# Spreading the reciprocals of the softmax sums over 128 partitions with Pool and TensorE in place of two DMAs, in an attention and mixture-of-experts kernel

## The chip, the core and the metric

The kernel runs on one core of one Trainium2 chip. A core has five engines that work side by side, each through its own instruction stream in order: TensorE (PE, with its weight load shown as PEld), VectorE (DVE), ScalarE (ACT), GpSimd (POOL) and SyncE (SP), which here only issues transfers. Sixteen DMA engines move data between the chip's memory and the core. An instruction that waits for a semaphore holds up all that stands behind it on its engine. The metric is the device time of one execution in microseconds (us).

## What is computed

Eight sequences of 512 tokens with 512 features go through a cross-attention with 16 heads of 32 features, and then through eight experts of which each takes its 512 best tokens. Cut to what matters:

```python
def xattn(q, k, v, mask, Wq, bq, Wk, bk, Wv, bv, Wo, bo):      # b=8, s=512, n=16 heads
    qh = (q @ Wq + bq).reshape(b, s, n, -1).transpose(0, 2, 1, 3)
    kh = (k @ Wk + bk).reshape(b, k.shape[1], n, -1).transpose(0, 2, 1, 3)
    vh = (v @ Wv + bv).reshape(b, v.shape[1], n, -1).transpose(0, 2, 1, 3)
    sim = einsum('bnid,bnjd->bnij', qh, kh) * 32 ** -0.5
    sim = where(~mask[:, None, None, :], finfo.min, sim)
    out = einsum('bnij,bnjd->bnid', softmax(sim, axis=-1), vh)
    return out.transpose(0, 2, 1, 3).reshape(b, s, -1) @ Wo + bo

x = x + xattn(layernorm(x), ctx, ctx, mask, ...)
x = x + ffn(layernorm(x), ...)     # softmax router, top 512 tokens of each of 8 experts, gelu, scatter-add
```

## The kernel before

The attention is worked off in 32 **groups**: a group is one sequence and four of its 16 heads, so four groups make a batch. Below, r0 to r3 are the four groups of a batch (`r = i % GB`), and g is a group's number. What a group takes, in the order of its data:

- The q and k projections, in three matmuls a chunk for accuracy (`hi` and `lo` parts; L1550 to L1552), are written by ACT and DVE to `qT_hi`, `qT_lo`, `kT_hi`, `kT_lo`. SP stores them to memory (`keep_hi` L735, `keep_lo` L742) and loads them back, stacked on other partitions, into `kst` and `qst` (`stack_hi` L758, `stack_lo` L767). A stack of q is three transfers of 256 KB. SP issues them in order, and the loads wait for the stores.
- Sixteen matmuls of kind `max` (L1564, tokens on partitions) give the scores of four heads and four token tiles. DVE takes each row's extreme (`nmax`, L1195), and ACT takes exp with its sum in `den` (`sum`, L1018). These wait for `qst` and `kst`.
- `rows`: PE turns the maxima to rows (L1571), ACT and DVE write them into `by_row` (L1009, L1203), and POOL copies them with two transfers into `qst` (`rows_lo`, L933).
- Sixteen matmuls of kind `score` (L1584, keys on partitions) give the scores again, with the maxima already subtracted. ACT takes exp (L1030), and four `att` steps multiply with v into `ps_att` (L1595).
- The sums' reciprocals are needed on the partitions of `ps_att`: head h and feature d on partition 32h + d, tokens along the free axis. `den` holds them as 128 tokens by 16 (head, tile). DVE takes the reciprocal (`recip`, L1211), PE turns it to 16 rows (`rden`, L1577), DVE copies the rows (L1218), POOL stores them to memory (`rden_rows`, L915), and POOL loads them back, each row for 32 partitions (`rden_in`, L924: 256 KB into `rden_b`). `divide` (L1228) multiplies `ps_att` with `rden_b` into `att_n`, which `osplit` turns into `oT_hi` and `oT_lo` for the output projection (L1611 to L1613).

Group i's scores run beside the maxima of group i + 1 and the projections of group i + 2. In between come the loads of the next sequence (r1), the first half of the output projection with its residual loads and `add_bias` on POOL (r2, L868 and L875), and the second half with the stores of x1, its normalisation and its routing (r0 of the next batch: `out`, `x1_norm`, `route`, `logits`, `back`; L1623 is the transposes of `route`).

The order is set by hand in `attention_agenda`: a group's time is cut into parts of 1/20, and a table gives the place at which each kind of step is put, as a fraction of a group (`K_AT`, `MAX_AT`, ...). PE works in that order. The other engines sort the same steps by their time plus a lag of their own (`a.lags`). Seven PSUM banks are given out in turn, so a step also waits until its bank has been emptied. After the attention comes the expert phase, which no part of the change touches.

## Time and profile before

| | |
|---|---|
| median of 3 runs | 1830.25 us (1829.41 to 1837.01) |
| the profiled execution, its own time | 1843.59 us |
| its span from first to last instruction | 1841.8 us |
| attention, between two like places of batches 0 and 7 (143.8 to 1012.0) | 868.2 us |
| PE, DVE, ACT busy in it | 774.5, 578.2, 668.5 us |
| experts (1090.0 to the end) | 751.8 us |

The profile lists for every engine how long it was busy, what it waited for, and which transfers it issued. PE's clock has two levels here, 1.2 and 2.4 GHz. The column PEclk is the mean granted clock as a share of the higher one, so 0.50 is a stretch wholly at 1.2 GHz. A wait "<-issue" is idle time for which the profile names no releaser.

### The profile page before, as it was taken

The page shows a single profiled execution, that of the slowest core. Times are in us where ns is not written, and L with a number is a line of the kernel's source. Part 1 is how long each engine was busy: PE and PEld are TensorE (multiplying, and loading weights), DVE is VectorE, ACT ScalarE, POOL GpSimd, SP SyncE. Part 2 cuts the span into 40 slices and gives each one's busy share as a digit, 9 for nine tenths or more (in the row PEclk, how much of TensorE's full clock was granted, in tenths as well). Part 3 has the DMA queues.
Part 4 walks back from the last instruction along what each step waited for, and adds up shares of the span by engine and source line. Part 5 has one row for each costly group of instructions (what it writes and reads, how often), then busy time and mean ns, then how long its engine had stood idle before and what let it go on. Part 6 is the DMA issues. An engine that isn't in the chain of part 4 may idle for free.

```text
span 1841.8 us, 22009 instructions
## 1 busy us (share of the span) xinstructions
PE 1642.2 (89%) x7667; PEld 1168.1 (63%) x7667; DVE 1112.4 (60%) x1950; ACT 982.2 (53%) x2111; POOL 309.1 (17%) x409
## 2 busy tenths in 40 slices
PE   4789989889789899898898629999999999999996
PEld 3545646546456456465564318878888888888885
DVE  5575775766656756767666455776544455554543
ACT  2687787778677776878878412222222232232321
POOL 3122121220221221212212111010202020202101
PEclk9789989889789899999998859999999999999998
DMA  5445462643644454627445122243425251525231
GB/s 187 127 125 143 132 165 73 195 111 104 179 112 126 149 133 134 164 79 213 118 136 156 65 80 89 72 121 115 146 89 166 69 166 69 166 71 178 86 107 23
DMA packets 142375, 227.53 MB, mean 124 GB/s; under 512 B 24380, under 2 KB 58832, under 8 KB 142264
## 3 DMA queue, kind: packets, MB, share of 16 engines
q1 hardware_dynamic: 115960, 175.85, 31.1%
q0 software_dynamic: 26304, 50.27, 10.7%
q8 instruction: 61, 1.00, 0.2%
q14 instruction: 50, 0.41, 0.1%
HBM read 166.36 MB, written 59.13 MB: 122 GB/s over the span
## 4 chain that ended last, share of the span: by engine, by line
PE 71%; DMA 12%; DVE 6%; ACT 6%; issue 3%; POOL 1%; SPq 0%; ACTq 0%; POOLq 0%; DVEq 0%
PE ps_gen L679 8%; PE ps_gen L680 8%; PE ps_gen L681 8%; PE ps_gen L1737 6%; PE ps_gen L1738 6%; PE ps_gen L1739 6%; PE ps_gen L1564 5%; PE ps_att L1595 5%; PE ps_gen L1584 4%; DMA qst<-qk_rows 4%; PE ps_gen L1550 3%; PE ps_gen L1551 3%; PE ps_gen L1552 3%; ACT ps_gen L1018 3%; DMA qk_rows<-qT_hi 2%
## 5 line engine op out<-in xcount | busy, mean ns | idle before, releaser
L1195 DVE TENSOR_REDUCE nmax<-ps_gen 128x1 f32<-128x512 f32 x512 | 340.3, 684 | 176.7 <-PE ps_gen L1564 172.1
L1030 ACT ACTIVATE p_ring<-ps_gen,keep_scale 128x512 f32<-128x512 f32 x512 | 336.3, 691 | 103.3 <-PE ps_gen L1584 103.2
L1018 ACT ACTIVATE ps_gen<-ps_gen,nmax 128x512 f32<-128x512 f32 x512 | 342.5, 672 | 90.1 <-DVE nmax L1195 89.8
L1080 ACT ACTIVATE gel<-ps_gen,b_cols 128x512 f32<-128x512 f32 x128 | 88.3, 690 | 451.4 <-PE ps_gen L681 451.3
L1564 PE MATMUL ps_gen<-kst,qst 97*128 97x512 f32 x512 | 226.6, 467 | 59.6 <-issue 30.0
L1449 DVE TENSOR_TENSOR gel_lo<-gel,gel_hi 128x512 fp32r<-128x512 f32 x126 | 87.2, 692 | 288.9 <-ACT gel_hi L1081 288.9
L1584 PE MATMUL ps_gen<-qst,kst 99*128 99x512 f32 x512 | 203.6, 449 | 26.5 <-ACT ps_gen L1018 13.7
L1564 PEld LDWEIGHTS ps_gen<-kst,qst 97*128 97x128 f32 x512 | 106.6, 212 | 157.3 <-issue 88.8
L679 PE MATMUL ps_gen<-hT_hi,w_hi 128*128 128x512 f32 x512 | 203.7, 398 | 1.5 <-DVE hT_lo L1442 1.5
L681 PE MATMUL ps_gen<-hT_hi,w_lo 128*128 128x512 f32 x512 | 200.8, 392 | 0.0
L680 PE MATMUL ps_gen<-hT_lo,w_hi 128*128 128x512 f32 x512 | 200.6, 392 | 0.0
L1737 PE MATMUL ps_gen<-w_hi,gel_hi 128*128 128x512 f32 x504 | 198.4, 394 | 0.0
L1739 PE MATMUL ps_gen<-w_hi,gel_lo 128*128 128x512 f32 x504 | 196.7, 390 | 0.0
L1738 PE MATMUL ps_gen<-w_lo,gel_hi 128*128 128x512 f32 x504 | 196.6, 390 | 0.0
L1595 PE MATMUL ps_att<-p_ring,v_sb 128*32 128x512 f32 x1024 | 154.2, 677 | 6.3 <-ACT p_ring L1030 6.3
L1584 PEld LDWEIGHTS ps_gen<-qst,kst 99*128 99x128 f32 x512 | 97.8, 206 | 90.0 <-issue 46.6
L959 POOL DMA_INDIRECT out_x<-y_out,idx x32 | 55.7, 1742 | 583.2 <-ACT y_out L1100 504.7
L1018 ACT ACTIVATION_READ_ACCUMULATOR ps_gen<-ps_gen,nmax 128x1 f32 x512 | 111.5, 218 | 0.0
L679 PEld LDWEIGHTS ps_gen<-hT_hi,w_hi 128*128 128x128 f32 x512 | 96.9, 189 | 21.2 <-issue 1.9
L681 PEld LDWEIGHTS ps_gen<-hT_hi,w_lo 128*128 128x128 f32 x512 | 96.8, 189 | 20.8
L680 PEld LDWEIGHTS ps_gen<-hT_lo,w_hi 128*128 128x128 f32 x512 | 97.0, 189 | 19.2
L1739 PEld LDWEIGHTS ps_gen<-w_hi,gel_lo 128*128 128x128 f32 x504 | 94.7, 188 | 19.8
(194 smaller groups left out, 2638.2 us busy)
## 6 DMA issues: line engine op xcount, KB each, us to landing
w_raw<-in_L_ffn_W SPq DMA_DIRECT2D x128, 512.0 KB, 5.0
kst<-qk_rows SPq DMA_DIRECT2D x96, 256.0 KB, 4.1
qst<-qk_rows SPq DMA_DIRECT2D x96, 256.0 KB, 4.7
x_in<-in_x POOLq DMA_DIRECT2D x60, 256.0 KB, 5.0
qk_rows<-kT_hi SPq DMA_DIRECT2D x32, 256.0 KB, 2.0
qk_rows<-kT_lo SPq DMA_DIRECT2D x32, 256.0 KB, 2.0
qk_rows<-qT_hi SPq DMA_DIRECT2D x32, 256.0 KB, 3.6
qk_rows<-qT_lo SPq DMA_DIRECT2D x32, 256.0 KB, 3.6
```

The source lines that it names most:

```text
L679: e.matmul(psum, lhsT=wh, rhs=mh, start=(i == 0), stop=False)
L680: e.matmul(psum, lhsT=wh, rhs=ml, start=False, stop=False)
L681: last = e.matmul(psum, lhsT=wl, rhs=mh, start=False, stop=(i == n - 1))
L1018: e.activation(psum[:, :], psum[:, :], ACT.Exp, bias=nmax[g % 2][:, c], scale=-1.0, accum_out=den[g % 2][:, c]).then_inc(drained_sem("max" ...
L1030: e.activation(p_ring[n % NP_][:, :], ps("score", g, kt, h)[:, :], ACT.Exp, scale=keep_scale[:, b:b + 1]).then_inc(drained_sem("score", g, ...
L1195: e.tensor_reduce(nmax[g % 2][:, h * TB + t:h * TB + t + 1], ps("max", g, h, t)[:, :], AX.X, ALU.min).then_inc(s_min, 1)
L1564: e.matmul(ps("max", g, h, t)[:, :], lhsT=qst[k][0:ROWS_MAX, h, t * P:(t + 1) * P], rhs=kst[k][0:ROWS_MAX, h, :], start=True, stop=True).t ...
L1584: e.matmul(ps("score", g, kt, h)[:, :], lhsT=kst[k][0:ROWS_ALL, h, kt * P:(kt + 1) * P], rhs=qst[k][0:ROWS_ALL, h, :], start=True, stop=Tr ...
L1595: last = e.matmul(ps_att[h * DH:(h + 1) * DH, :], lhsT=v_sb[:, kt, (c4 * HG + h) * DH:(c4 * HG + h + 1) * DH], rhs=p_ring[((g * KT + kt) * ...
L1737: e.matmul(ps_y[tt], lhsT=gh, rhs=wh, start=(j == 0), stop=False)
L1738: e.matmul(ps_y[tt], lhsT=gh, rhs=wl, start=False, stop=False)
L1739: return e.matmul(ps_y[tt], lhsT=gl, rhs=wh, start=False, stop=(j == NF - 1))
```

## The change

Three things are changed.

First, the reciprocals no longer go through memory. POOL copies `rden` (128 tokens by 16) into a new tile `rden_wide` (128 by 4 by 128) and repeats each element 32 times along the free axis. PE then turns its four 128x128 blocks by transposes, and since each head's value stands 32 times along the free axis, it now stands on 32 partitions. DVE copies the whole bank of 128x512 into `att_n`, and `divide` reads and writes `att_n` in place. `rden_b`, `rden_rows`, both transfers of each group and the semaphores `s_rd_out` and `s_rd_in` are gone.

Second, there are other waits: `recip` on DVE waits for POOL's copy of the group before, POOL's copy waits for `recip`, PE's transposes wait for POOL's copy, and DVE's copy waits for `osplit_lo` of the group before, since it overwrites `att_n`.

Third, the places and lags of the table are set anew.

```diff
-    ROWS_AT = 0.74
-    RECIP_AT, RDEN_AT, RDEN_IN_AT, OSPLIT_AT = -0.07, 0.28, 0.63, 0.17
+    ROWS_AT = 0.70
+    RECIP_AT, RDEN_AT, OSPLIT_AT = 0.02, 0.50, 0.15
-    LOAD_X_AT, STATS_X_AT = (0.32, 0.63), (0.62, 0.99)
+    LOAD_X_AT, STATS_X_AT = (0.12, 0.47), (0.65, 0.96)
-    HALF_AT, HALF_FOR = (("residual", 0.20), ("add_bias", 0.35), ("outa", 0.49)), 0.78
+    HALF_AT, HALF_FOR = (("residual", 0.05), ("add_bias", 0.23), ("outa", 0.48)), 0.78
...
-        place(i, (RDEN_IN_AT, RDEN_IN_AT), [(a.add, "rden_in", i)])
...
-        rden_b = sb(p1, "rden_b", [P, S])
+        rden_wide = sb(p1, "rden_wide", [P, TB, P])
...
+                elif kind == "recip":
+                    g, = at
+                    on.wait_ge(s_ones_rows[NST - 1], 2)
+                    on.wait_ge(s_rden, g + 1)
+                    if g > 0:
+                        on.wait_ge(*full("rden", g - 1))
+                    e.tensor_copy(rden_wide[:, :, :].rearrange("p t (h d) -> p t h d", d=DH),
+                                  rden[:, :].rearrange("p (h t d) -> p t h d", t=TB, d=1).to_broadcast([P, TB, HG, DH])
+                                  ).then_inc(s_rden_wide, 1)
...
-                elif kind == "rden":
-                    g, = at
-                    on.wait_ge(*drained("rden", g))
-                    if g >= 2:
-                        on.wait_ge(s_rd_in, 16 * (g - 1))
-                    e.dma_start(rden_rows[g % 2].rearrange("h (t n) -> (h t) n", n=P), rd_rows).then_inc(s_rd_out, 16)
-
-                elif kind == "rden_in":
-                    g, = at
-                    on.wait_ge(s_rd_out, 16 * (g + 1))
-                    on.wait_ge(s_mask_store, 16)
-                    if g > 0:
-                        on.wait_ge(s_nrm, g)
-                    src = rden_rows[g % 2].rearrange("h (r n) -> h r n", r=1).to_broadcast([HG, DH, S])
-                    e.dma_start(rden_b[:, :], src).then_inc(s_rd_in, 16)
...
-                    if g > 0:
-                        on.wait_ge(s_rd_out, 16 * g)
-                    e.tensor_copy(rd_rows, ps("rden", g)[0:HG * TB, 0:P]).then_inc(drained_sem("rden", g), 1)
+                    if g == 0:
+                        on.wait_ge(s_mask_store, 16)
+                    else:
+                        on.wait_ge(s_ol, g)
+                    e.tensor_copy(att_n[:, :], ps("rden", g)[:, :]).then_inc(drained_sem("rden", g), 1)
...
-                    on.wait_ge(s_rd_in, 16 * (g + 1))
-                    if g > 0:
-                        on.wait_ge(s_oh, g)
-                        on.wait_ge(s_ol, g)
-                    e.tensor_tensor(att_n[:, :], ps_att[:, :], rden_b[:, :], ALU.mult).then_inc(s_nrm, 1)
+                    on.wait_ge(*drained("rden", g))
+                    e.tensor_tensor(att_n[:, :], ps_att[:, :], att_n[:, :], ALU.mult).then_inc(s_nrm, 1)
...
-                    on.wait_ge(s_rden, g + 1)
-                    e.transpose(ps("rden", g)[0:HG * TB, 0:P], rden[:, :], ident[:, :]).then_inc(full_sem("rden", g), 1)
+                    on.wait_ge(s_rden_wide, g + 1)
+                    for t in range(TB):
+                        last = e.transpose(ps("rden", g)[:, t * P:(t + 1) * P], rden_wide[:, t, :], ident[:, :])
+                    last.then_inc(full_sem("rden", g), 1)
```

On POOL, in r2 of the first batch, the order before was this (`x_in<-in_x` is a residual load, `x_in<-x_in,bo_b` its `add_bias`, `qst<-by_row` is `rows_lo`):

```order
L868 DMA x_in<-in_x 128x512
L915 DMA rden_rows<-by_row 16x128
L875 TENSOR_TENSOR x_in<-x_in,bo_b 128x512
L868 DMA x_in<-in_x 128x512
L924 DMA rden_b<-rden_rows 128x1x512
L875 TENSOR_TENSOR x_in<-x_in,bo_b 128x512
L868 DMA x_in<-in_x 128x512
L933 DMA qst<-by_row 1x16x128 x2
L875 TENSOR_TENSOR x_in<-x_in,bo_b 128x512
```

At the same place it is now this:

```order
L873 COPY rden_wide<-rden 128x512
L865 DMA x_in<-in_x 128x512
L882 TENSOR_TENSOR x_in<-x_in,bo_b 128x512
L865 DMA x_in<-in_x 128x512
L882 TENSOR_TENSOR x_in<-x_in,bo_b 128x512
L865 DMA x_in<-in_x 128x512
L882 TENSOR_TENSOR x_in<-x_in,bo_b 128x512
L924 DMA qst<-by_row 1x16x128 x2
```

The copy stands ahead of the residual loads, both transfers of the reciprocals are gone from between them, and the third `add_bias` now comes ahead of `rows_lo`.

On PE, in r2 of the fifth batch, this is what followed the last q projection (first row) before. `ps_gen<-qst,kst` is a `score`, `ps_gen<-kst,qst` a `max` of the next group:

```order
L1552 MATMUL ps_gen<-xT_hi,wq_lo 128x512
L1584 MATMUL ps_gen<-qst,kst 128x512
L1564 MATMUL ps_gen<-kst,qst 128x512
L1584 MATMUL ps_gen<-qst,kst 128x512
L1564 MATMUL ps_gen<-kst,qst 128x512 x2
L1584 MATMUL ps_gen<-qst,kst 128x512 x2
L1564 MATMUL ps_gen<-kst,qst 128x512
L1595 MATMUL ps_att<-p_ring,v_sb 32x512 x4
L1564 MATMUL ps_gen<-kst,qst 128x512
```

Now it is this:

```order
L1542 MATMUL ps_gen<-xT_hi,wq_lo 128x512
L1554 MATMUL ps_gen<-kst,qst 128x512
L1576 MATMUL ps_gen<-qst,kst 128x512
L1554 MATMUL ps_gen<-kst,qst 128x512 x2
L1576 MATMUL ps_gen<-qst,kst 128x512
L1554 MATMUL ps_gen<-kst,qst 128x512 x2
L1576 MATMUL ps_gen<-qst,kst 128x512 x2
L1568 MATMUL ps_gen<-ident,rden_wide 128x128 x4
L1554 MATMUL ps_gen<-kst,qst 128x512
L1587 MATMUL ps_att<-p_ring,v_sb 32x512 x4
L1554 MATMUL ps_gen<-kst,qst 128x512
```

The last q projection is two `max` matmuls earlier in the order, and the four transposes stand behind it, where before the single one stood ahead of it. What comes after these rows, up to the first `max` for which PE needs the stack of this q, is the same in both.

## Rows read from the trace of the kernel before

**Rows 1.** The page's part 1: busy time by engine, its share of the span.

```profile
PE 1642.2 (89%) x7667; PEld 1168.1 (63%) x7667; DVE 1112.4 (60%) x1950; ACT 982.2 (53%) x2111; POOL 309.1 (17%) x409
```

**Rows 2.** Windows: stretch, its us, busy PE, PEld, DVE, ACT, POOL; PEclk, DMA share, GB/s.

```profile
143.83:1012.00 868.17, 774.51 (x3650) 482.85 (x3649) 578.18 (x1110) 668.45 (x1550) 175.57 (x286) 0.92 0.49 138
392.12:521.87 129.75, 114.62 (x526) 71.84 (x524) 84.21 (x162) 95.75 (x222) 25.49 (x41) 0.88 0.46 131
772.42:891.62 119.20, 106.29 (x526) 67.10 (x524) 83.36 (x162) 95.25 (x222) 25.31 (x41) 0.97 0.51 143
```

**Rows 3.** Waits of PE in 143.83 to 1012: us in total, times, longest.

```profile
PE ps_gen L1564 <- issue: 27.7, 14, 3.8
PE ps_gen L1564 <- ACT ps_gen L1018: 17.7, 15, 1.7
PE ps_gen L1584 <- DMA qst<-by_row: 9.7, 10, 3.0
PE ps_gen L1564 <- DMA qst<-qk_rows: 1.9, 2, 1.1
```

**Rows 4.** Timeline of PE: start, us, instruction, idle time before it.

```profile
279.14 0.77 PE L1564 MATMUL ps_gen<-kst,qst 97*128 97x512 f32 x1 [2.65 <-issue]
342.66 0.47 PE L1564 MATMUL ps_gen<-kst,qst 97*128 97x512 f32 x1 [2.20 <-issue]
406.18 0.76 PE L1564 MATMUL ps_gen<-kst,qst 97*128 97x512 f32 x1 [3.84 <-issue]
845.65 0.70 PE L1564 MATMUL ps_gen<-kst,qst 97*128 97x512 f32 x2 [1.14 <-DMA qst<-qk_rows]
```

**Rows 5.** Windows of 8 us that begin where such waits end, columns as in rows 2.

```profile
279.14:287.14 8.00, 8.00 (x22) 6.35 (x23) 3.59 (x7) 3.62 (x10) 2.13 (x3) 0.61 0.14 35
342.66:350.66 8.00, 7.68 (x25) 4.42 (x26) 4.37 (x9) 3.45 (x9) 1.70 (x3) 0.57 0.47 163
785.18:793.18 8.00, 8.00 (x37) 5.65 (x38) 5.26 (x9) 5.57 (x14) 2.60 (x3) 1.00 0.13 35
```

**Rows 6.** Timeline of POOL's and SP's queues in r2, 266 to 271.

```profile
267.37 0.70 POOL L924 DMA_DIRECT2D rden_b<-rden_rows  x1 [0.98 <-DMA rden_rows<-by_row]
...
269.88 0.80 SPq L758 DMA_DIRECT2D qst<-qk_rows  x2
```

**Rows 7.** DMA issues of 269.86 to 270.78, us to landing at the end.

```profile
qst<-qk_rows SPq DMA_DIRECT2D x3, 256.0 KB, 7.7
```

**Rows 8.** The same of 680.14 to 681.06, in r3.

```profile
qst<-qk_rows SPq DMA_DIRECT2D x3, 256.0 KB, 8.1
```

**Rows 9.** The same of 921.80 to 922.70, in r3.

```profile
qst<-qk_rows SPq DMA_DIRECT2D x3, 256.0 KB, 3.7
```

**Rows 10.** The same of 803.06 to 803.98, in r3; `rden_b` was issued at 801.58.

```profile
qst<-qk_rows SPq DMA_DIRECT2D x2, 256.0 KB, 5.8
```

**Rows 11.** Timeline of POOL's queue, issues of `rden_b` by rows 8 and 9.

```profile
679.30 0.72 POOL L924 DMA_DIRECT2D rden_b<-rden_rows  x1 [2.01 <-DMA rden_rows<-by_row]
922.48 0.72 POOL L924 DMA_DIRECT2D rden_b<-rden_rows  x1 [3.54 <-issue]
```

**Rows 12.** Timeline of PE: four transposes of 128x128, and the single one of `rden`.

```profile
610.33 0.60 PE L1623 MATMUL ps_gen<-ident,x_in 128*128 128x128 f32 x4
614.48 0.27 PE L1577 MATMUL ps_gen<-ident,rden 128*16 128x128 f32 x1
```

**Rows 13.** Groups of instructions on POOL and DVE: count, busy us, mean ns, idle before.

```profile
L875 POOL TENSOR_TENSOR x_in<-x_in,bo_b 128x512 f32<-128x512 f32 x32 | 41.0, 1281 | 43.7 <-DMA x_in<-in_x 43.4
L1245 DVE COPY hnT<-ps_gen 128x512 f32<-128x512 f32 x28 | 19.3, 689 | 22.7 <-PE ps_gen L1623 22.7
L1218 DVE COPY by_row<-ps_gen 16x128 f32<-16x128 f32 x32 | 9.0, 282 | 2.1 <-PE ps_gen L1577 0.6
```

**Rows 14.** Timeline of DVE and POOL at 15 us, where both work on SBUF.

```profile
15.17 2.11 DVE L1120 TENSOR_SCALAR x_in<-x_in,mv,rstd 128x512 f32<-128x512 f32 x1 [0.66 <-POOL rstd L811]
15.19 1.80 POOL L845 MEMSET kst<- 32x2048 f32 x1
```

41 lines of the change are left out of this document (19 added, 22 removed).

## The prediction

> **What bounds the kernel now.** I read the busy times first [rows 1]: PE is busy for 1642.2 of 1841.8 us, and every other engine for 60% or less. Then the stretch in which the change lies, by windows [rows 2]. In 868.17 us of attention PE is busy for 774.51, ACT for 668.45 and DVE for 578.18 us. So PE sets the pace there, and what can be won is its 93.7 us of idle time and what its clock costs (0.92 of full). A slow batch takes 129.75 us at clock 0.88 and a quick one 119.20 us at 0.97, with the same instructions in the same order: idle time and clock are the whole difference.
>
> Next, PE's waits in that stretch [rows 3]. The matmul at L1564 waits 27.7 us for "issue" in 14 pieces and 1.9 us for the stack transfer by name. The timeline shows where [rows 4]: at the first `max` of a group, in r2 (at 279.14 and 406.18, five more of 1.9 to 3.5 us) and in r0 (at 342.66 and 845.65, six in all, 0.8 to 2.2 us). Both lie where a stack of q has just landed: the three loads issued from 269.88 on took 7.7 us [rows 6, 7], so they landed at about 278.5, and PE went on at 279.14. I take these "issue" waits as waits for the stack. Another 9.7 us are waits for `rows_lo`. The 17.7 us at L1564 for ACT are bursts of ACT's own work in r1 and r2, and this change does not touch them.
>
> The clock comes on top. In the 8 us after such a wait it was 0.61 and 0.57, so PE spent most of them at 1.2 GHz, while ACT was busy for under 4 of the 8 us and so did not hold PE up [rows 5]. After the waits of the quick batch it stayed at 1.00. Of the twelve such windows from 279 us on, eight are below 1: together they lose 22.5 us ((1 - clock) times 8 each).
>
> **What the change removes.** No wait of `divide` on `rden_b` shows in the trace, so its transfer costs nothing by itself. What it costs is its place among other transfers. `rden_b` is issued at 267.37, 2.5 us ahead of the stack for which PE then waits [rows 6]. r3 shows the price with little else in flight: with `rden_b` issued at 679.30, ahead of the stack, the stack took 8.1 us; issued at 922.48, behind it, 3.7 us [rows 8, 9, 11]. So up to 4.4 us per stack. Another stack with it ahead took 5.8 us [rows 10], which gives 2.1 us as the low end. The waits in r2 sum to 18.9 us (seven) and those in r0 to 8.6 us (six). With 2.1 us off each, at least 14.5 and 8.5 us of them would go, 23 in all; with 4.4 us all 27.5. But residual loads in r2 and the stores of x1 in r0 remain among these transfers, so part of the relief is lost. In r2 the last q projection also moves two `max` matmuls earlier against the first matmul that needs it, which adds half a microsecond or more of slack. I take **24 us** of gain, with 10 as the low end if the remaining loads take the freed place.
>
> The waits for `rows_lo` (9.7 us) follow in the same stretches and pass POOL's queue, on which two issues per group are gone. In r1 the loads of x are placed earlier, so its normalisation no longer stands late ahead of `rows_lo`. I take **4 us**, ends 0 and 9.7.
>
> The clock: if a wait shrinks below about 1 us, the stretch after it has a chance to stay at 2.4 GHz, as after the 1.14 us at 845.65 [rows 4]. The profiled execution had 22.5 us of this loss, but its own time, 1843.59 us, is 13.3 us above the median, and I put that down to the clock. A median run then has about 9 us of it left to win, of which I take **6**; ends 0 and 22.5, the latter against the profiled run's own time.
>
> **What it adds.** On PE, four transposes stand where one did. Four of 128x128 took 0.60 us from first start to last end, one took 0.27 us [rows 12]. The difference of 0.33 us in 32 groups is **11 us**, and PE has no cover for it outside its waits. At 1.2 GHz it is near twice that, so the ends are 11 and 22. A rule of the Trainium skill speaks for a higher price: "TensorE: Matmul & The Clock Gate", section "PE-mode transpose", gives about 275 ns for one 128x128 transpose in a kernel. The single one here agrees (0.27 us), but four in a row overlap: 0.60 us, not 1.1 us. By the page's figure for each of the four the term would be 26 us instead of 11, and the forecast some 15 us later.
>
> On DVE, a copy of 689 ns takes the place of one of 282 ns [rows 13]: 0.41 us times 32 is 13 us more on an engine that is idle for a third of the stretch. It costs where DVE is late for the next `nmax`, and PE's bank is held by it: 1 us, ends 0 and 5. On POOL the copy of 128x512 is an operation the trace does not show. The nearest row is `add_bias` of that size with 1281 ns [rows 13]. It comes at 0.06 of a group and PE asks at 0.50, some 12 us later, and POOL is busy for 20% of the time, so it is hidden; only for the first group does the chain from `recip` over POOL to PE lie open. There PE waits for `rows_lo` anyway: 1 us. `divide` waits for DVE's own copy half a group earlier: nothing.
>
> **The sum.** -24 - 4 - 6 + 11 + 1 + 1 = -21 us, so 1830.25 becomes **1809 us**. The places that are moved besides shift single steps by a place or two on PE, and I give them no term.
>
> **The rivals.**
>
> *All of it comes back.* Both kinds of waits and the clock recover nearly whole: -27.5 - 9.7 - 22.5 + 13 = -46.7 against the profiled run's own time of 1843.59, so some 1797, and less for a median run whose clock also gains: 1785 to 1797. For it speaks the quick batch of 119.20 us; against it that the quick batch still had its waits, so a part of the spread between batches has another cause.
>
> *The freed place is taken.* `rden_b` is one of several transfers before each late stack. If residual loads and x1 stores now meet the stack, relief is half (-12), the clock does not recover, `rows_lo` gives nothing: -12 + 13 = +1, 1831 us, no difference that the measurement can tell. About 0.5% of the time is what it can tell.
>
> *POOL stands in DVE's way.* At 15.17 a DVE operation of this shape took 2.11 us while POOL wrote `kst` beside it [rows 14], where even a copy of that size out of PSUM takes 0.69 us [rows 13]. POOL's new copy runs at the start of each group, and in r1 and r2 a normalisation, on which the transposes for `route` and of x wait, stands close to it. If each of these 14 is held up by the 1.3 us of a copy and passes it on to PE, 18 us are lost: 1830.25 - 21 + 18 = 1827 us. "SBUF — State Buffer", section "Who interferes with whom", in the Trainium skill states this as a rule: a DVE operation in a two-port mode and one of GpSimd exclude each other for a whole instruction. The trace agrees at that one place; no row shows it inside the groups.
>
> *PE pays and wins nothing (slower).* The waits in r2 are set by the chain store, load, landing of q alone, and `rden_b`'s share is hidden behind the residual loads. Then PE carries four transposes in each group, and where the clock is at 1.2 GHz for double the price: +11 to +22 and 2 for the rest, 1843 to 1854 us. The point from which it decides is a relief of less than the price of the transposes, 0.35 to 0.7 us per group, or 1.4 to 2.8 us per batch where a batch now waits some 4 us for stacks. Against it speaks the pair in r3, for it that in r2 residual loads are in flight too.
>
> **How the numbers follow.** Forecast (1797 to 1821): 0.50. All of it: 0.18. Freed place: 0.14. POOL in DVE's way: 0.06. PE pays: 0.12. Faster by over 0.5% (below 1821.1) 0.68, within 0.5% 0.20, slower by over 0.5% (above 1839.4) 0.12. The range reaches from the lower end of the second case to the near end of the slower one: 1785 to 1842. It leaves out most of the slower case and a tail below.
>
> **What would show it.** In the profile after: 64 fewer issues on POOL's queue; the stack of q in r2 lands in 4 to 6 us instead of 7 to 8; the waits at L1554 for "issue" and the stack fall from 29.6 us to under 8; PE's clock in the attention rises from 0.92 to 0.94 or more; the four transposes at L1568 take 0.6 us at 2.4 GHz, and PE never waits for POOL's copy; DVE's copy into `att_n` takes 0.69 us; the expert phase keeps its 752 us. I am wrong if the stack still takes over 7 us in r2, if new waits appear at the transposes or at L1554 for ACT above the 17.7 us, or if PE's clock does not rise though the waits are gone.

## The result, and the profile after

| | before | after |
|---|---|---|
| median of 4 runs each | 1833.14 us (1829.41 to 1837.01) | 1774.47 us (1772.48 to 1778.16) |
| ratio to before | | 0.9676, 95% interval 0.9646 to 0.9706 |
| the profiled execution, its own time | 1843.59 us | 1773.36 us |
| its span | 1841.8 us | 1771.6 us |
| six batches, `divide` of group 3 to `divide` of group 27 | 744.8 us | 687.4 us |
| from the last `divide` to the end | 809.3 us | 807.6 us |

The changed kernel is 58.7 us faster. The forecast was 21 us, and the measured time lies below the stated range of 1785 to 1842. The direction was right, the size was not. Since 57.4 us of the difference lie in the six batches, the rest of this text reads that stretch. Between two `divide`s lies one group, so the `divide`s also give the time of each group (means over six batches, worked out from their starts in the timeline of DVE):

| group | before | after |
|---|---|---|
| r0 | 33.0 | 30.9 |
| r1 | 32.0 | 27.5 |
| r2 | 33.0 | 29.9 |
| r3 | 26.2 | 26.2 |

Line numbers of after are about ten lower than before: the `max` matmuls stand at L1554 (before L1564), the `score` matmuls at L1576 (L1584), the transposes of the reciprocals at L1568 (L1577). The page of after begins with this line of busy times, which answers [rows 1]:

```profile
PE 1612.9 (91%) x7763; PEld 1152.6 (65%) x7763; DVE 1119.6 (63%) x1950; ACT 982.6 (55%) x2111; POOL 293.3 (17%) x377
```

PE has 96 instructions more (three transposes in each of 32 groups) and is nevertheless busy for 29 us less, at a granted clock of 0.960 over the whole execution where it was 0.931. POOL has 32 fewer: 64 issues are gone and 32 copies came. The windows, with columns as in [rows 2]: first before and then after over the six batches, then r1 of the second of the six batches, before and after.

```profile
191.90:936.67 744.77, 665.01 (x3145) 416.64 (x3146) 502.09 (x966) 572.90 (x1327) 152.43 (x240) 0.93 0.49 137
```

```profile
180.57:867.99 687.42, 644.12 (x3218) 405.37 (x3217) 507.61 (x968) 573.57 (x1327) 141.47 (x217) 0.98 0.48 139
```

```profile
348.31:380.63 32.32, 28.14 (x127) 15.72 (x128) 25.07 (x55) 25.00 (x60) 8.04 (x14) 0.81 0.51 145
```

```profile
326.79:354.03 27.24, 23.41 (x122) 12.70 (x122) 23.78 (x54) 24.32 (x58) 7.50 (x13) 0.94 0.59 170
```

Two things fall together. PE's idle time goes from 744.77 - 665.01 = 79.8 us to 687.42 - 644.12 = 43.3 us, and its granted clock rises from 0.93 to 0.98. The waits of PE in the two stretches (us in total, times, longest), first before:

```profile
PE ps_gen L1564 <- issue: 23.7, 12, 3.8
PE ps_gen L1564 <- ACT ps_gen L1018: 16.2, 13, 1.7
PE ps_gen L1584 <- ACT ps_gen L1018: 10.7, 24, 0.8
PE ps_gen L1584 <- DMA qst<-by_row: 7.7, 8, 3.0
```

and after:

```profile
PE ps_gen L1568 <- ACT ps_gen L1009: 10.4, 12, 1.2
PE ps_gen L1576 <- ACT ps_gen L1009: 9.6, 20, 0.9
PE ps_gen L1561 <- DVE nmax L1186: 8.5, 12, 1.6
PE ps_gen L1554 <- ACT ps_gen L1009: 5.0, 12, 0.6
...
PE ps_gen L1576 <- DMA qst<-by_row: 1.7, 3, 0.8
```

The 23.7 us for "issue" at the first `max` are gone altogether, and `rows_lo` fell from 7.7 to 1.7 us. The waits for ACT have moved and not shrunk: those at the `max` matmuls fell from 16.2 to 5.0 us, but the transposes now wait 10.4 us for ACT to empty their PSUM bank, where the single transpose of before waited for nothing in its six batches. All waits for ACT at PSUM banks that the two answers list add up to 26.9 us before (16.2 and 10.7) and 26.6 us after (10.4, 9.6, 5.0 and 1.6 at the k and q projections). In the chain that ended last, DMA had 12% of the span and has 3%. The stack of q in r2, which took 7.7 us before [rows 7] (7.1 to 8.1 in the six batches), now takes this (us from issue to landing at the end of the line), and 3.5 to 4.0 us in all six:

```profile
qst<-qk_rows SPq DMA_DIRECT2D x3, 256.0 KB, 3.7
```

The clock by group, as the mean over six windows weighted by their length, with the two runs e1 (the new mechanism in the old table) and e3 (before without the transfers), which are told below:

| PE's granted clock | before | e3 | e1 | after |
|---|---|---|---|---|
| r0 | 0.95 | 1.00 | 1.00 | 1.00 |
| r1 | 0.83 | 0.86 | 0.86 | 0.92 |
| r2 | 0.93 | 1.00 | 0.99 | 1.00 |
| r3 | 1.00 | 1.00 | 1.00 | 1.00 |

The three added operations: four transposes on PE in the timeline of after (start, us, instruction), which answers [rows 12], the copy on DVE from the groups of instructions (busy us, mean ns), and the copy on POOL from the answer for its line (shortest, median, longest ns in the window 100 to 300).

```profile
625.41 0.60 PE L1568 MATMUL ps_gen<-ident,rden_wide 128*128 128x128 f32 x4
```

```profile
L1211 DVE COPY att_n<-ps_gen 128x512 f32<-128x512 f32 x32 | 21.8, 682 | 5.3 <-PE ps_gen L1568 5.3
```

```profile
L873 POOL COPY rden_wide<-rden x7: 604/611/616, 124.0 to 295.5; 128x512 f32<-128x512 f32 x7
```

### The profile page after: what moved, and what is told of

It reads as the page before. It is cut to its first block, busy times and chain, and to the rows that moved or that the text cites. A ratio compares the mean times of both kernels' runs of the same rounds, so it can differ in the third digit from the quotient of the medians.

```text
span 1771.6 us, 22168 instructions
## 1 busy us (share of the span) xinstructions
PE 1612.9 (91%) x7763; PEld 1152.6 (65%) x7763; DVE 1119.6 (63%) x1950; ACT 982.6 (55%) x2111; POOL 293.3 (17%) x377
## 4 chain that ended last, share of the span: by engine, by line
PE 78%; DVE 9%; ACT 8%; DMA 3%; issue 2%; POOL 1%; SPq 0%; POOLq 0%; DVEq 0%; ACTq 0%
PE ps_gen L676 8%; PE ps_gen L677 8%; PE ps_gen L678 8%; PE ps_gen L1729 7%; PE ps_gen L1730 6%; PE ps_gen L1731 6%; PE ps_gen L1554 5%; PE ps_att L1587 5%; PE ps_gen L1576 5%; ACT ps_gen L1009 4%; PE ps_gen L1540 3%; PE ps_gen L1541 3%; PE ps_gen L1542 3%; ACT p_ring L1021 2%; DVE stat L1102 2%
## 5 line engine op out<-in xcount | busy, mean ns | idle before, releaser
L1554 PE MATMUL ps_gen<-kst,qst 97*128 97x512 f32 x512 | 216.0, 440 | 19.1 <-ACT ps_gen L1009 8.7
L1576 PE MATMUL ps_gen<-qst,kst 99*128 99x512 f32 x512 | 194.4, 429 | 18.4 <-ACT ps_gen L1009 12.9
L1554 PEld LDWEIGHTS ps_gen<-kst,qst 97*128 97x128 f32 x512 | 99.8, 198 | 99.3 <-issue 58.8
L1587 PE MATMUL ps_att<-p_ring,v_sb 128*32 128x512 f32 x1024 | 145.5, 642 | 3.3 <-ACT p_ring L1021 3.1
L1576 PEld LDWEIGHTS ps_gen<-qst,kst 99*128 99x128 f32 x512 | 94.0, 195 | 78.6 <-ACT ps_gen L1009 30.2
```

The lines of the kernel that those rows point to most:

```text
L1554: e.matmul(ps("max", g, h, t)[:, :], lhsT=qst[k][0:ROWS_MAX, h, t * P:(t + 1) * P], rhs=kst[k][0:ROWS_MAX, h, :], start=True, stop=True).t ...
L1576: e.matmul(ps("score", g, kt, h)[:, :], lhsT=kst[k][0:ROWS_ALL, h, kt * P:(kt + 1) * P], rhs=qst[k][0:ROWS_ALL, h, :], start=True, stop=Tr ...
L1587: last = e.matmul(ps_att[h * DH:(h + 1) * DH, :], lhsT=v_sb[:, kt, (c4 * HG + h) * DH:(c4 * HG + h + 1) * DH], rhs=p_ring[((g * KT + kt) * ...
```

## The experiments

Two theories stood after the result. **A** (T in the expectations): the removal of the transfers is worth more than I gave it, and the places are worth little. **B** (P in the expectations): the places, to which I gave no term, carry a large part. A third one was that the new operations cost less than 13 us. Every experiment was timed beside the kernel before on the same chip, whose medians there were 1829.4 to 1831.5 us. There were four chips: one for e1 to e4, one for e5 to e8, one for e9 to e12, one for e13 to e15. I put differences across chips, and those to the changed kernel, at an uncertainty of some 5 us. That is an estimate from the intervals of the table.

| run | what it is | median us | ratio to before, 95% interval |
|---|---|---|---|
| e1_old_places | new mechanism, old places | 1796.26 | 0.9804 (0.9765 to 0.9842) |
| e2_new_places | old mechanism, new places | 1860.25 | 1.0168 (1.0115 to 1.0221) |
| e3_no_transfers | before, transfers left out | 1784.32 | 0.9745 (0.9704 to 0.9785) |
| e4_load_early | before, load at an earlier place | 1858.86 | 1.0145 (1.0102 to 1.0187) |
| e5_split_as_before | after, splits' places undone | 1782.12 | 0.9738 (0.9711 to 0.9765) |
| e6_eight | after, eight transposes | 1784.74 | 0.9747 (0.9716 to 0.9777) |
| e7_rden_as_before | after, reciprocals' places undone | 1784.90 | 0.9756 (0.9727 to 0.9784) |
| e8_proj_max_as_before | after, projections' and maxima's undone | 1774.14 | 0.9691 (0.9663 to 0.9718) |
| e9_both_as_before | e5 and e7 together | 1789.41 | 0.9770 (0.9743 to 0.9797) |
| e10_new_places_rden_old | before, new places, reciprocals' old | 1801.56 | 0.9843 (0.9810 to 0.9876) |
| e11_r2_as_before | after, projections of r2 undone | 1774.73 | 0.9694 (0.9668 to 0.9720) |
| e12_load_put_back | after, a load of the removed shape put back | 1799.04 | 0.9818 (0.9775 to 0.9861) |
| e13_x_as_before | after, places of the loads of x undone | 1790.13 | 0.9786 (0.9722 to 0.9850) |
| e14_three_as_before | e5, e7 and e13 together | 1806.82 | 0.9881 (0.9817 to 0.9945) |
| e15_rden_late | e1, reciprocals at their new place | 1803.30 | 0.9867 (0.9802 to 0.9932) |

### The change taken apart: mechanism, places, transfers

**e1_old_places** is the changed kernel with the whole table of before. The copy on POOL takes the lag 0.08. Of the table, this is the line of the reciprocals against the changed kernel:

```diff
...
-    RECIP_AT, RDEN_AT, OSPLIT_AT = 0.02, 0.50, 0.15
+    RECIP_AT, RDEN_AT, OSPLIT_AT = -0.07, 0.28, 0.17
...
```

> The new way of spreading the reciprocals (POOL's copy, four transposes, no transfers) with the places and lags of the kernel before; the single new lag puts POOL's copy 0.01 of a group after the group's start. Theory T (the transfers of the reciprocals held up the stacks of q, and the clock fell behind each wait): the waits of PE for stacks fall from 29.6 us to under 6 and the time to 1775 to 1800 us, most of the 58 us. Rival P (the places do it): the waits for ACT in r1 stay, stacks still come late, and the time is 1820 to 1840 us.

**e2_new_places** is the kernel before with the new table. The load keeps its place 0.63. Against before:

```diff
...
-    RECIP_AT, RDEN_AT, RDEN_IN_AT, OSPLIT_AT = -0.07, 0.28, 0.63, 0.17
+    RECIP_AT, RDEN_AT, RDEN_IN_AT, OSPLIT_AT = 0.02, 0.50, 0.63, 0.15
...
```

> The kernel before, with both transfers of the reciprocals at 0.51 and 0.56 of a group, and all other places and lags of the changed kernel. Theory T: the stacks still stand behind the 256 KB load, 1815 to 1835 us. Rival P: 1775 to 1795 us, since the places alone spread ACT's splits in r1 and bring forward the loads.

**e3_no_transfers** is the kernel before without the store and the load of the reciprocals from group 1 on. What waited for a group's own store or load waits for those of the first group instead.

```diff
                 elif kind == "rden":
                     g, = at
+                    if g > 0:
+                        continue
...
                 elif kind == "rden_in":
                     g, = at
+                    if g > 0:
+                        continue
...
-                        on.wait_ge(s_rd_out, 16 * g)
+                        on.wait_ge(s_rd_out, 16)
...
-                    on.wait_ge(s_rd_in, 16 * (g + 1))
+                    on.wait_ge(s_rd_in, 16)
```

> The kernel before with its own places; both transfers of the reciprocals are left out from the second group on, so all groups divide by the sums of the first and the output is not the reference's. Nothing is added to PE, DVE or POOL. Theory T: stack of q in r2 lands in 4 to 6 us instead of 7 to 8, waits for stacks under 6 us, 1770 to 1795 us, some 10 us below e1_old_places, by the three transposes more that that one has. Rival P: 1820 to 1835 us.

Measured beside 1831.13 us of before: leaving the transfers out alone gives 1784.32 (-46.8), the whole new mechanism 1796.26 (-34.9). So the engines' new work costs 11.9 us against 13 forecast. The new places on top of the mechanism bring it from 1796.3 to 1774.5 (-22). The same places with the old mechanism make it 29 us slower. Each theory holds in part: the removal was worth 13 us more than forecast (A), and the places 22 us where I had nothing (B). The windows over the six batches, first e1 and then e3:

```profile
182.22:888.99 706.77, 650.54 (x3217) 413.42 (x3218) 508.19 (x966) 571.16 (x1327) 136.94 (x216) 0.96 0.46 135
```

```profile
182.26:878.07 695.81, 640.40 (x3145) 402.68 (x3146) 500.30 (x967) 570.94 (x1327) 124.29 (x192) 0.96 0.47 137
```

The clock is 0.96 in both, half way between before and after. Before and e3 have the same 3145 recorded matmuls in their six batches, so the windows divide what the removal gave into waits and clock. The six batches are 49.0 us shorter. PE's idle time fell from 79.8 to 55.4 us, which is 24.4 us, and its busy time from 665.0 to 640.4 us, which is 24.6 us for the same work at the higher clock. Over the whole execution idle time fell by 27.0 us and busy time by 34.3 us, 61.3 us in all. That is 14.5 us more than the medians differ: the profiled execution of before lies 12.5 us above the median beside e3, and that of e3 2.1 us below its own. If all of these 14.5 us are clock, the removal gave a median run about 27 us of waits and 20 us of clock (an estimate from these figures). PE's waits in e1:

```profile
PE ps_gen L1554 <- ACT ps_gen L1009: 16.1, 13, 1.7
PE ps_gen L1576 <- ACT ps_gen L1009: 10.7, 24, 0.8
PE ps_gen L1561 <- DVE nmax L1186: 6.1, 12, 0.7
PE ps_gen L1576 <- DMA qst<-by_row: 5.5, 4, 1.9
```

The waits for stacks are gone with the transfers alone (in e3 0.9 us of them are left, and 2.3 us for `rows_lo`). The waits for ACT at PSUM banks are as long in e1 (16.1 and 10.7 us) as in before and after. By groups, e1 has 31.3, 31.2, 28.8 and 26.4 us in r0 to r3. The mechanism wins in r2 (33.0 to 28.8) and r0, the places win in r1 (31.2 to 27.5), where idle time is 1.3 us and busy time 2.4 us a group less than in e1. In the six batches idle time falls by 12.9 us from e1 to after: the waits for `hnT` (5.8 us), for `p_ring` (4.0), for `probs` (3.3) and for `xT_lo` (1.3) go or shrink beside those for `rows_lo` (3.8), while those at L1561 and for `qT_lo` grow by some 4 us.

Why does e2 lose? Both expectations missed it, at 1860 us. Its waits of PE over the six batches begin with this:

```profile
PE ps_gen L1584 <- DMA qst<-by_row: 27.7, 17, 2.9
```

The waits for the stacks are gone here too, with both transfers still in place: wherever the load was issued near a stack of q, it came 3.6 us or more behind it, and the stacks of r2 took 3.5 to 3.8 us. But the waits for `rows_lo` rose from 7.7 to 27.7 us. The six batches took 744.9 us, as in the profiled execution of before (744.8), which lies above its median; the last batch, to its last `divide`, took 107.9 us instead of 95.8, with 11.1 us of the same wait. POOL's queue in r1 shows the reason (timeline of e2: start, us, instruction, idle time before it):

```profile
243.95 0.51 POOL L915 DMA_DIRECT2D rden_rows<-by_row  x1
248.84 0.71 POOL L924 DMA_DIRECT2D rden_b<-rden_rows  x1 [4.37 <-DMA rden_rows<-by_row]
249.56 0.57 POOL L811 TENSOR_TENSOR rstd<-rstd,half 128x1 f32<-128x1 f32 x1
250.10 1.20 POOL L933 DMA_DIRECT2D qst<-by_row  x2
```

With the reciprocals at 0.50 of a group the load comes right behind its store, POOL waits 4.37 us for the store to land, and `rows_lo` stands behind it in the queue. PE then waits 2.72 us for it, at 254.35. The changed kernel has neither the store nor the load, so this wait is not there.

**e10_new_places_rden_old** tests that: the kernel before with the new places, but the reciprocals where they were. Of the table, this line stays as it is in before, and the others are the new ones:

```diff
...
     RECIP_AT, RDEN_AT, RDEN_IN_AT, OSPLIT_AT = -0.07, 0.28, 0.63, 0.17
...
```

> The kernel before with the new places, but with its own places and lags for reciprocal, transpose and osplit, so the rows are stored at 0.29 instead of 0.51 of a group. If the 29 us that the new places cost the old way come from POOL's store, load and rows_lo being crowded together at 0.51 to 0.71: 1800 to 1830 us, at or below the kernel before. If they come from elsewhere (residual loads before the stack): 1850 to 1865 us.

1801.56 beside 1830.59: 29 us faster than before with both transfers still there. So the loss of e2 lies in the reciprocals' place, and the other new places are worth 29 us even to the old mechanism. This is the strongest result against my step. Two of its waits show that these places relieve in part what the removal relieves:

```profile
PE ps_gen L1584 <- DMA qst<-by_row: 12.7, 11, 2.5
...
PE ps_gen L1564 <- issue: 5.2, 6, 1.5
```

The waits for stacks are 5.2 us here, against 24.8 us in before (23.7 and 1.1). In r2 the load is now issued 0.2 to 2.2 us behind the stack and no longer ahead of it, and the stack takes 3.6 to 5.6 us. So the two gains are not independent, and the removal has no single price. With the old table it gave 34.9 us net (before to e1). With the new table and the reciprocals at their old place it gave about 17 us (e10, 1801.56, to e7 below, 1784.90), and with the whole new table 86 us (e2 to after).

### Are the transfers what costs?

**e4_load_early** asks whether the load would only have needed a better place: the kernel before, with the load placed ahead of q's stores.

```diff
-    RECIP_AT, RDEN_AT, RDEN_IN_AT, OSPLIT_AT = -0.07, 0.28, 0.63, 0.17
+    RECIP_AT, RDEN_AT, RDEN_IN_AT, OSPLIT_AT = -0.07, 0.28, 0.44, 0.17
```

> The kernel before with one number changed: the load of the spread reciprocals is placed at 0.44 instead of 0.63 of a group (0.37 with its lag), ahead of the stores of q instead of between them and the stack; the transfers are all there. Theory T, in its form that the position of the load among the transfers is what costs: 1790 to 1815 us. If it is the bytes and packets themselves, wherever they stand, or if the wait moves to the loads of k: 1825 to 1840 us. Rival P: no change, 1828 to 1838 us.

1858.86 us, 1.5% slower. PE's waits show that the cost only moved:

```profile
PE ps_gen L1564 <- issue: 16.1, 12, 2.9
PE ps_gen L1564 <- ACT ps_gen L1018: 15.7, 15, 1.7
PE ps_gen L1584 <- DMA qst<-by_row: 13.6, 13, 2.0
...
PE ps_gen L1564 <- DMA qst<-qk_rows: 6.5, 5, 1.8
```

The waits for stacks stay at 16.1 + 6.5 = 22.6 us, and those for `rows_lo` rise from 7.7 to 13.6. The load did not come clear of the stacks: in five of the six r2 it was still issued 0.4 to 1.1 us ahead of the stack, which took 7.9 to 8.7 us. In the sixth it came 1.8 us behind, and the stack took 3.9 us. So e4 says nothing on a load that is out of the way. e2 and e10 do: with the load behind the stack, the stack is quick.

**e12_load_put_back** puts into the changed kernel what was taken out: a load of 256 KB in rows for 128 partitions from memory, on POOL's queue near its old place. Its data are not used. It waits on POOL for PE's transposes, and POOL's next copy waits for it.

```diff
+            place(i, (0.63, 0.63), [(a.add, "extra", i)])
...
+                elif kind == "extra":
+                    g, = at
+                    on.wait_ge(*full("rden", g))
+                    on.wait_ge(s_mask_store, 16)
+                    src = raw(mask_rows[0:HG, :]).rearrange("h (r n) -> h r n", r=1).to_broadcast([HG, DH, S])
+                    e.dma_start(rden_wide[:, :, :].rearrange("p t n -> p (t n)"), src).then_inc(s_extra, 16)
...
                 elif kind == "recip":
                     g, = at
+                    if g > 0:
+                        on.wait_ge(s_extra, 16 * g)
...
```

> The changed kernel with one load of 256 KB put back in each group but the last, of the shape of the one removed (four rows of memory, each for 32 partitions) and at its place (0.56 on POOL), into rden_wide after the transposes have read it; nobody uses what it brings, and POOL's next copy waits for it. Theory T (this load among the others held up the stacks and the rows): 25 to 50 us more, 1800 to 1825 us, with waits for stacks or rows_lo again. If the transfers only mattered through the waits that hung on them (store, load, POOL's order): under 8 us more, below 1782 us.

1799.04 us, 24.6 more than the changed kernel and just below what theory T gave. PE's waits in its six batches hold two that after has hardly or not at all (`score` at L1588 and `max` at L1566 here):

```profile
PE ps_gen L1588 <- DMA qst<-by_row: 11.9, 10, 3.1
...
PE ps_gen L1566 <- issue: 4.7, 5, 3.6
```

The clock fell from 0.98 to 0.96. In the six batches idle time rose by 10.2 us and busy time by 11.0 us. In them no wait of POOL's copy ends with this load; over the whole execution one does. A rival is that the load holds `rows_lo` up in POOL's queue, and not on its way. The trace decides in r1, where most of the longer waits are. `rows_lo` is issued as soon as its row is written in both kernels, but behind a load issued some 3 us earlier it takes 2.4 to 4.1 us to land, where after has 1.7 to 1.9. In the first of the six batches, first e12 and then after:

```profile
qst<-by_row POOLq DMA_DIRECT2D x2, 8.0 KB, 3.1
```

```profile
qst<-by_row POOLq DMA_DIRECT2D x2, 8.0 KB, 1.8
```

In r0, with the load 2.5 us ahead, the stack takes 5.6 to 6.3 us instead of 3.7 to 3.9. In r2 the load comes 1.4 us behind the stack, which takes 3.6 us or less. So one load per group costs 0.8 us a group, by the other transfers that it delays and by the clock. In this run the delay falls on `rows_lo` more than on the stacks, so it is no copy of what happened in before. The store and the wait of the load for it are not in it.

### Where the places pay

Each of these is the changed kernel with one or more sets of places and lags as before (the last one, e15, starts from e1). The lags that belong to a set are changed with it and are left out of the cuts below.

**e5_split_as_before:** the splits of the next sequence's context on ACT and DVE (`cT_hi`, `cT_lo`), in r1.

```diff
-    LOAD_C_AT, SPLIT_C_AT = (-0.25, 0.15), (0.28, 0.52)
+    LOAD_C_AT, SPLIT_C_AT = (-0.26, 0.06), (0.34, 0.49)
...
```

> The changed kernel with only the places and lags of the splits of the next sequence's context (and the place of its loads) as before: ACT's four splits in r1 stand in pairs between fewer exps. Theory S (the 22 us by which the changed kernel is quicker than the new way with the old places are ACT's burst in r1): r1 goes back from 27.5 towards 31 us a group, 1788 to 1800 us. Rival R (it is the later place of the transposes, or the projections' and maxima's places): 1774 to 1780 us.

**e7_rden_as_before:** `recip`, the transposes and `osplit`.

```diff
-    RECIP_AT, RDEN_AT, OSPLIT_AT = 0.02, 0.50, 0.15
+    RECIP_AT, RDEN_AT, OSPLIT_AT = -0.07, 0.28, 0.17
...
```

> The changed kernel with reciprocal, transposes and osplit at their places of before (-0.07, 0.28, 0.17; POOL's copy at 0.01): the transposes stand in the first third of a group. Theory S: 1772 to 1780 us. Rival R in its first form: 1785 to 1800 us.

**e8_proj_max_as_before:** `K_AT`, `Q_AT`, `MAX_AT` and `ROWS_AT`. **e11_r2_as_before:** of the first three only r2's.

```diff
-    K_AT = ((0.01, 0.34), (-0.04, 0.22), (0.06, 0.16), (-0.12, 0.08))
-    Q_AT = ((0.41, 0.43), (0.20, 0.28), (0.21, 0.32), (0.20, 0.33))
-    MAX_AT = ((-0.12, 0.59), (-0.07, 0.66), (-0.04, 0.62), (-0.17, 0.60))
-    ROWS_AT = 0.70
+    K_AT = ((-0.02, 0.39), (0.05, 0.22), (0.05, 0.16), (-0.07, 0.12))
+    Q_AT = ((0.42, 0.42), (0.22, 0.28), (0.18, 0.37), (0.12, 0.34))
+    MAX_AT = ((-0.12, 0.59), (-0.07, 0.66), (-0.12, 0.62), (-0.17, 0.58))
+    ROWS_AT = 0.74
```

> The changed kernel with the places of projections, maxima and rows as before. Theory S: 1774 to 1784 us, with r1 at 27 to 28 us a group. Rival R in its second form: 1788 to 1800 us.

> The changed kernel with the projections' and maxima's places of r2 alone as before. With all of them as before, r2 took 28.3 us instead of 29.9 a group and r1 28.7 instead of 27.5, with the same total. If the gain belongs to r2's places and the loss to the others': 8 x 1.6 = 13 us less, 1760 to 1767 us, below both kernels. If r1's loss hangs on the same numbers (the maxima of r2 begin in r1): 1772 to 1778 us.

**e9_both_as_before:** e5 and e7 together.

> The changed kernel with both the splits' and the reciprocals' places as before. Alone they cost 7.6 and 10.4 us. If they are separate causes and the rest of the table (projections, maxima, loads of x, lags) is worth little, the sum stands: 1788 to 1797 us, about the 1796 us of the new way with all old places. If they are one cause, the burst in r1, seen twice: 1782 to 1787 us.

**e13_x_as_before:** the loads, statistics and normalisation of x and the residual loads with their `add_bias`.

```diff
-    LOAD_X_AT, STATS_X_AT = (0.12, 0.47), (0.65, 0.96)
-    NORM_X_AT, TURN_X_AT = (0.71, 1.08), (0.96, 1.15)
-    HALF_AT, HALF_FOR = (("residual", 0.05), ("add_bias", 0.23), ("outa", 0.48)), 0.78
+    LOAD_X_AT, STATS_X_AT = (0.32, 0.63), (0.62, 0.99)
+    NORM_X_AT, TURN_X_AT = (0.66, 1.08), (0.97, 1.16)
+    HALF_AT, HALF_FOR = (("residual", 0.20), ("add_bias", 0.35), ("outa", 0.49)), 0.78
...
```

> The changed kernel with the places and lags of the loads of x, its statistics and normalisation, and of the residual loads with their add_bias, all as before. The places are worth 22 us with the new mechanism, of which the reciprocals' and the splits' places explain 15. Theory 'the loads of x and of the residual hold the rest': some 7 us slower than the changed kernel (1774.5), that is 1779 to 1784. Rival 'the rest lies in the lags and the output projection's places': 1773 to 1777.

**e14_three_as_before:** e5, e7 and e13 together. **e15_rden_late:** e1 with the reciprocals' new place.

> The changed kernel with three sets of places as before: reciprocals, splits, and the loads of x and of the residual. If these three hold all that the places are worth, it lands at the new mechanism with the old places, 1796 (1793 to 1799). If what is left lies elsewhere, it lands with the first two alone, 1789 (1787 to 1791).

> The new mechanism with all old places (1796.3), except that the reciprocals, their transposes and osplit take the new places. Theory 'the late place of the transposes is worth its 10 us by itself': 1785 to 1788. Rival 'it pays only together with the splits' new place' (the bursts of ACT in r1 stay): 1791 to 1797.

Against 1774.5 us the splits are worth 7.6, the reciprocals' place 10.4, both together 15 (e9), the places of x 15.6, the projections and maxima nothing (-0.3). In e8 and e11 r2 gains 1.6 us and r1 gives 1.2 to 1.7 back. Several of these times lie outside what I had expected: e5 between its two theories, e7 just below its rival, e13 and e14 above both of their ranges, e15 above both too.

Do the parts add up? The three sets do: 7.6 + 10.4 + 15.6 = 33.6, and all three together (e14) cost 32.3. What does not fit is the rest of the table. e14 has three sets old and the rest new, e1 has everything old, and e1 is 10 us faster, though by e8 a good part of the rest, the projections, maxima and `rows`, is worth nothing in the new table. How much of the 10 us is real is open: the two runs are from different chips, their intervals just meet, and their profiled executions differ by only 2.5 us in the six batches (709.2 and 706.8). The late transposes in the old table (e15) bring nothing (1803.3 beside 1796.3 of e1, intervals that overlap, and 707.1 and 706.8 us in the six batches), where the same step is worth 10 in the new table. So a set has the price that was measured here only in the table in which it was measured.

What such a place does can in part be read. **ACT's splits in r1.** In before, in r1 of the second of the six batches, the timeline of ACT holds the four splits among the exps at 361.45, 362.17, 363.92 and 365.10, the first two with only a small exp of the router between them:

```profile
361.45 0.63 ACT L985 ACTIVATE cT_hi<-x_in 128x512 fp32r<-128x512 f32 x1
362.03 0.23 ACT L1052 ACTIVATE probs<-probs 128x32 f32<-128x32 f32 x1
362.17 0.61 ACT L985 ACTIVATE cT_hi<-x_in 128x512 fp32r<-128x512 f32 x1
```

PE waits next (timeline of PE). In the 8 us up to 364 the clock was 1.00, and the 8 us from there run at 1.2 GHz throughout:

```profile
364.07 1.22 PE L1564 MATMUL ps_gen<-kst,qst 97*128 97x512 f32 x2 [1.73 <-ACT ps_gen L1018]
```

```profile
364.00:372.00 8.00, 7.13 (x25) 2.62 (x25) 6.44 (x13) 8.00 (x22) 3.50 (x6) 0.50 0.94 232
```

After, in r1 of the same batch, the splits start at 335.52, 337.63, 339.57 and 340.76, with at least one exp of the softmax between any two. PE's single waits there are shorter, and the 8 us from the last split on have the clock 0.79:

```profile
338.97 0.73 PE L1576 MATMUL ps_gen<-qst,kst 99*128 99x512 f32 x2 [0.84 <-ACT ps_gen L1009]
340.91 1.06 PE L1568 MATMUL ps_gen<-ident,rden_wide 128*128 128x128 f32 x4 [1.21 <-ACT ps_gen L1009]
```

```profile
340.76:348.76 8.00, 7.01 (x31) 2.96 (x32) 7.79 (x18) 7.88 (x21) 3.21 (x6) 0.79 0.81 237
```

e5 sets back only the splits. PE's idle time in its six batches is 43.0 us, as in after (43.3), and all of the difference is clock: in r1 the clock is 0.88 instead of 0.92, and busy time is 0.9 us a group longer. That a wait of 1.7 us in place of two shorter ones is what lowers the clock is my reading of these places, and no run tests it alone.

**The reciprocals.** In e7 the waits of L1554 for ACT are back, in place of those of the transposes (16.0 us against 5.0 and 10.4 in after). What is new are the waits of the transposes of `route` for the normalisation on DVE, which are 0.8 us in after:

```profile
PE ps_gen L1554 <- ACT ps_gen L1009: 16.0, 24, 1.2
PE ps_gen L1615 <- DVE x_in L1111: 7.9, 12, 1.1
```

So PE's wait for ACT is there with either place, and at 0.50 the transposes stand where it falls. That the waits of `route` carry the 10 us is not shown.

**The places of x.** The timeline of DVE in e13, r1 of the third of the six batches, from the first statistics of x on. L1194 is DVE's part of `rows`, for which `rows_lo` on POOL's queue waits:

```profile
464.61 0.69 DVE L1102 BATCH_NORM_STATS2 stat<-x_in 128x6 f32<-128x512 f32 x1 [0.74 <-DMA x_in<-in_x]
...
466.40 0.55 DVE L1111 TENSOR_SCALAR x_in<-x_in,mv,rstd 128x512 f32<-128x512 f32 x1 [0.69 <-POOL rstd L808]
466.98 0.28 DVE L1194 SCALAR_TENSOR_TENSOR by_row<-ps_gen,by_row 16x128 fp32r<-16x128 f32 x1
```

and the same place in after:

```profile
460.50 0.68 DVE L1102 BATCH_NORM_STATS2 stat<-x_in 128x6 f32<-128x512 f32 x1
...
461.61 0.28 DVE L1194 SCALAR_TENSOR_TENSOR by_row<-ps_gen,by_row 16x128 fp32r<-16x128 f32 x1
...
463.18 0.59 DVE L1111 TENSOR_SCALAR x_in<-x_in,mv,rstd 128x512 f32<-128x512 f32 x1
```

In e13 the row's write stands behind the first normalisation, which waits for x to land and then for POOL's `rstd`; in after it stands ahead of it. `rows_lo` is issued 5.2 us after the last load of x instead of 3.2, and PE pays. The `score` matmul in e13:

```profile
470.19 1.19 PE L1576 MATMUL ps_gen<-qst,kst 99*128 99x512 f32 x2 [2.53 <-DMA qst<-by_row]
```

It does so in each of the six batches, for 0.33 to 2.53 us, 8.8 us in all against 1.7 in after, and r1 takes 29.5 us instead of 27.5. The kernel before and e1 have the same order on DVE in each r1: statistics, normalisation with its wait for POOL, then the row. There PE waits for `rows_lo` in r1 too, 0.3 to 3.0 us in four of the six batches of before and 0.9 to 1.9 us in three of e1. The other 4 us or so by which e13's idle time is above that of after, and its 4.7 us more of busy time, are not traced.

### What the transposes cost

**e6_eight** does each of the four transposes twice.

```diff
-                    for t in range(TB):
+                    for t in 2 * list(range(TB)):
```

> The changed kernel with each of the four transposes made twice, so eight instead of four in a group. By the prediction's price (0.11 us for each further transpose, no cover on PE): 32 x 0.44 = 14 us more, 1788 us. If the waits of PE at this place cover them: under 5 us more. If each costs the 0.27 us of a single one: 35 us more, 1809 us.

1784.74 us, 10.3 more for 128 transposes: 0.08 us each, in a kernel where PE is 91% busy. The three more per group of the change are then worth 96 x 0.08 = 7.7 us. The 11.9 us between e3 and e1 leave some 4 for DVE's longer copy and for what PE, DVE and POOL pass on to each other.

## Why the prediction was wrong, step by step

Two steps failed. The places, which got no term, were worth 22 us. The clock, of which I took 6 us, gave the removal alone about 20. The waits that the removal was to end were sized right.

**What bounds the kernel:** right. PE sets the pace, and its idle time and clock were what could be won. All 57 us of the six batches came from there: idle time fell by 36.5 us, and busy time by 20.9 us, in spite of 73 more recorded matmuls in that stretch.

**"I take 24 us of gain" for the stacks:** right in mechanism and near in size. In e3 the waits for stacks in the six batches fell from 24.8 to 0.9 us, and in e1 none is left in the list. The stack of q went from 7.7 to 3.7 us, at the upper of my two bounds (4.4 us a stack). I had taken a part off for "residual loads in r2 and the stores of x1 in r0 remain among these transfers, so part of the relief is lost". Nothing was lost, so the term should have been the whole 27.5 us, 3.5 more.

**"I take 4 us" for `rows_lo`:** right at its place for the mechanism: 7.7 us before, 5.5 us in e1 (2.3 in e3), 1.7 us only with the new places. Together with the stacks I had 28 us of waits. PE's idle time fell by 27.0 us in e3, over the whole execution.

**"of which I take 6" for the clock: the first failed step, a mis-sized term.** I took the profiled run's 13.3 us over the median to be clock, subtracted it from 22.5, and took two thirds of the 9 us that were left. The removal shortened PE's busy time by 24.6 us in the six batches of e3 for the same recorded matmuls. Less the 14.5 us by which the profiled pair differs more than the medians, the 34.3 us of the whole execution are still about 20 us. I had counted windows only behind the waits for stacks, in r0 and r2. There all was won (from 0.95 and 0.93 to 1.00), and r1, which I had not counted, rose from 0.83 to 0.86. Nor is a wait's length alone the sign that I took it for: behind the 2.54 us wait at 785.18 the clock stayed at 1.00 [rows 5], behind one of 1.22 us at 598.96 it was 0.57. The whole sum for the removal was -34, measured -46.8.

**"+11, +1, +1" for the new work:** right. 11.9 measured between e1 and e3, of which 7.7 are transposes by e6. Four took 0.60 us at 2.4 GHz, as the row of another line had said. Per transpose the whole kernel paid 0.08 and not 0.11 us.

**"shift single steps by a place or two on PE, and I give them no term": the second failed step, and the largest error.** The places are worth 22 us with the new mechanism (1796.3 to 1774.5). I looked only at PE's order, in which they are small. On ACT and DVE a place decides what stands ahead of an instruction that PE waits for. Two such pairs were there to be read in the trace of before: the adjacent splits on ACT ahead of the 1.73 us wait in r1, and the row's write behind a normalisation on DVE. Of the 17.7 us at L1564 for ACT I had written that "this change does not touch them". At that line it did, but the waits for ACT as a whole stayed (26.9 and 26.6 us in the six batches). What the places gave lies in shorter waits for `rows_lo`, `hnT`, `p_ring` and `probs`, 12.9 us less idle time than in e1, and in the clock of r1 (0.86 to 0.92). Nor did I see that the late place of the reciprocals costs more than it gives while the transfers are there (e2 against e10), or that the new places relieve the stacks on their own (e10).

**The rivals.** "All of it comes back" named 1785 to 1797. e1, the mechanism by itself, is 1796.3, so of the mechanism alone this rival was the better description: it had all waits and all of the clock's 22.5 us. The time of the whole change lies beyond it by the places, which it left out too. "The freed place is taken" is refuted by e1 and e3. "POOL stands in DVE's way" did not come about: POOL's copy takes 0.61 us, half of the 1.28 us by which I bounded it, and in the timelines of after none of the 32 copies runs beside a normalisation. In the answer for the normalisation's line (shortest, median, longest ns) one of 64 is long, at 15.14 us, ahead of the first copy:

```profile
L1111 DVE TENSOR_SCALAR x_in<-x_in,mv,rstd x64: 535/539/2106, 5.5 to 982.1; 128x512 f32<-128x512 f32 x64
```

The Trainium skill, "SBUF — State Buffer", section "Who interferes with whom", lets such a pair exclude each other when they meet. No row of the six batches shows a meeting, so these runs neither support nor contradict it there. "PE pays and wins nothing" had its point at a relief of 1.4 to 2.8 us a batch. The removal of the transfers alone gave 46.8 us in eight batches, 5.9 us each.

**What the profile was to show.** 64 fewer issues: yes. Stack in 4 to 6 us: 3.7, even lower. Waits at L1554 for issue and stack under 8: between 100 and 960 us one of 1.0 us is left. Clock 0.94 or more: 0.98 in the six batches. Four transposes 0.6 us: yes. DVE's copy 0.69: 0.68. Experts unchanged: 809.3 and 807.6 us after the last `divide`. "PE never waits for POOL's copy": once, in the first group, for 4.23 us, where I had given 1 us:

```profile
63.69 1.09 PE L1568 MATMUL ps_gen<-ident,rden_wide 128*128 128x128 f32 x4 [4.23 <-POOL rden_wide L873]
```

And one sign that I had set for being wrong came up, new waits at the transposes (10.4 us for ACT). They stand in place of waits that PE had at the `max` matmuls, and the time with the transposes at their old place (e7) is 10 us longer.

**What stays open.** The 22 us of the places are traced to sets (e5, e7, e13), and two of them to a pair of instructions by reading and not by a run of its own. Together the three sets are worth 32 us in the new table, so with them set back the rest of the new table costs some 10 us, if the comparison across two chips holds; which part does, and why, is open. The removal's division into some 27 us of waits and 20 us of clock is measured in one pair of profiled executions and carried over to the medians by an estimate. e12 shows the load without its store, and with its delay on `rows_lo` more than on the stacks.

## What to carry to other kernels

A small result that goes through memory and back costs more than its own waits: look at what else is on its way, and behind it in the same queue, in those microseconds, and price the clock beside the waits: here it was about 20 of 47 us. When a diff sets a table of places anew, read the order of every engine around each wait of the bounding engine, above all two long operations in a row on the engine that it waits for, and price the table as a set: undo it whole first, and only then in parts. A mechanism and a table can relieve the same wait, so the price of either holds only beside the other: here the new way gave about 17, 35 or 86 us, depending on the table. Once a mechanism no longer needs a round trip, its old place may no longer be the best one, so try the two together.
